# Flamingo block on Trainium2: the first layer's routing in two bursts, its scatters from iteration 18 on, the second routing and the weight fold moved to the attention's end and the first expert blocks

## The chip, the cores and the metric

The kernel runs on one core of a Trainium2 chip. The metric is the device time of one execution in microseconds (us); the times shown are medians of a few executions. Five engines work side by side and meet only at semaphores: TensorE (PE, matmuls), VectorE (DVE), ScalarE (ACT), GpSimd (POOL) and SyncE (SP), which issues most of the DMAs. Each engine runs its instructions in the order of its program, so a wait at the head holds up all that is queued behind it.

## The reference, cut to what matters

Two layers run on x of shape (128, 64, 128), 8192 tokens of 128 numbers, with a context of the same size. The change touches the first layer and the step from its attention to its experts:

```python
x = x + tanh(g_xattn[0]) * L0_xattn(layernorm(x), ctx)      # 16 heads of 8
# L0_ffn on layernorm(x): each token goes to its best 2 of 8 experts
logits = xt @ Wg + bg
scores = softmax(logits); topk_probs, topk_idx = top_k(scores, 2)
h = gelu(xt @ W1[e] + b1[e]); eo = h @ W2[e] + b2[e]
out = topk_probs[:, 0] * eo[topk_idx[:, 0]] + topk_probs[:, 1] * eo[topk_idx[:, 1]]
x = x + tanh(g_ffn[0]) * out
# layer 1: masked attention with one head, then experts that choose their 17 best tokens of each row of 64
```

All arithmetic shown is float32.

## The kernel before

**Tiles and parts.** The tokens are 64 tiles of 128. The first layer's expert stage treats them in three parts, tiles 0 to 23, 24 to 47 and 48 to 63. For each part the tokens are sorted by expert in DRAM: an indirect DMA per tile and per choice (`put`) writes the normalised rows to their places in `xg`, the expert blocks read `xg` in order, and indirect DMAs (`get`) fetch the results back. Part 0 has 17 blocks of 256 rows and 21 of 128.

**Attention of layer 0.** A loop over p = 0 to 34 treats two tiles in each iteration, as a pipeline of four stages. In iteration p PE does `scores(p)` and `attend(p-2)`, `spread_rden(p-3)`, `output(p-3)`; DVE does `largest(p)` (line 1173, the maximum over 128x2048), `normalise(p-3)` (1191), `shift(p)` (1179), `add_output(p-3)` (1197), `stats0` and `stats_router` (1164, 1169), `invert(p-2)` (1185). `scores(p+1)` needs the banks that `shift(p)` reads. ACT does the exponentials, copies the sums of stage p-2 (`copy_sums`, 1695), and at the end of iteration p normalises two tiles of group p//2+2 (`norm0`, 1709). SP moves the sums by DMA (`move_sums(p)`, 482 and 485), and behind them in iteration p it loads weights and writes two pieces of zeros (`fill`, 470) into `xg` and `odd`. There are 38 pieces, so the last two belong to p = 18. `move_sums(18)` waits for the sums that ACT copies in its iteration 20.

**POOL in that loop.** In an even p it spreads the keys of group p//2+1 (`keys`, 1973), which `scores(p+2)` reads; in every p it adds a bias to two tiles (`add_bias`, 1988); for p = 3, 7, 11, ... it computes mean and deviation (`moments_twice`, 1953 to 1963, and `moments`, 1928 to 1937); then come the puts (1999) of this p. `norm0(12)` in ACT's iteration 20 waits for the moments of POOL's iteration 19. Each `put` begins with

```python
                w.wait_ge(s_fill, 16 * fills)
                w.wait_ge(s_place, TOP * (h + 1))
```

**Routing.** `route0(h)` on DVE is a generator that the loop advances by hand: logits, softmax (its exponential on ACT), the two best experts, counts (`count0`, two matmuls on PE, copied by ACT), the block table, the place of each token, the expert of each block. Part 0 is routed in iterations 17 to 22 and its tiles are put in POOL's iterations 23 to 34; part 1 is routed in iterations 29 to 34 and put after the loop; part 2 is routed in the first expert blocks. The weights of layer 1 are folded on PE and DVE in iterations 33 and 34 (`output_bias`, `multiply_weights`, `fold_weights`).

**Expert blocks.** For each block PE turns the next unit's tokens (849), does `up0` (859) and, one block later, `down0` (869); DVE copies the turned tokens (1367), adds the bias (1386), in the small blocks copies weights (1377), and has steps of routing, of later rows (1158) and of combining between them.

Of the kernel before, what the change touches and what calls it, by code (L numbers as in the profile page):

```python
# [6 lines left out]

# [4 lines left out]
ALU = mybir.AluOpType  # L12
# [6 lines left out]
P = 128  # L19
# [60 lines left out]
UP_BANKS, DOWN_BANKS = (0, 1, 2, 5), (3, 6)  # L80
# [3 lines left out]
ROWS_FROM = 22  # L84
ROWS_BY = (3, 5, 6, 8, 9, 11, 12, 14, 15, 17, 20, PARTS[0][1])


def rows_by(p):

    return ROWS_BY[min(p - ROWS_FROM, len(ROWS_BY) - 1)] if p >= ROWS_FROM else 0  # L90
# [5 lines left out]
ROUTE1_FROM = 7  # L96

# [93 lines left out]
def build(nc, t_in, out):  # L191
    with ExitStack() as ctx:
# [106 lines left out]
        bias_rows = [ln1[:, 0, :], cut(9984, dict(d=D), "d")]  # L299
# [52 lines left out]
        def vec(name, n=1):  # L352
# [5 lines left out]
        BIAS_BANKS, ROUTER_BANKS = (0, 7), (1, 2, 3)  # L358
# [28 lines left out]
            "s_sm", "s_ex", "s_ch", "s_count", "s_counted", "s_place", "s_expert")]  # L387

# [41 lines left out]

        def routing_start(h):
            return 2 * (sum(PARTS[h]) // TG - 1) + 7
# [8 lines left out]
        def sync_program(e):  # L441
# [45 lines left out]

            filling = fill()
# [12 lines left out]
            def fetch_weights(b):  # L501
                _, h, j, _, _ = BLOCKS[b]
                w.wait_ge(s_expert, h + 1)
                number = e.value_load(expert[0:1, h, j:j + 1], min_val=0, max_val=NE - 1)
                w.wait_ge(ld["w1"], 16 * NE)
                w.wait_ge(s_hg, HC * (b - NW + 1))
                w.wait_ge(s_yb, b - NW + 1)
                e.dma_start(w1g(b), w1_sb[:, bass.ds(number, 1), :].rearrange("p a n -> p (a n)")
                            ).then_inc(s_w1g[b % NW], 16)
# [19 lines left out]
            w.wait_ge(s_sc, NP)  # L529
            w.wait_ge(s_kx, NG)  # L530
            for b in range(AHEAD):
                fetch_weights(b)
            for i in range(2):
                w.wait_ge(s_pt, 4 * (NP - 1 + i))
                half = slice(i * NE // 2, (i + 1) * NE // 2)
                load("w2", w2_sb[:, half], t_in["w2a"][:, half])
            w.wait_ge(s_bm, 2)
# [52 lines left out]
        def tensor_program(e):  # L590
# [8 lines left out]
            def output_bias(layer, weights):  # L599
                w.wait_ge(s_bv, layer + 1)  # L600
                wait_bank(BIAS_BANKS[layer])
                e.matmul(banks[BIAS_BANKS[layer]][:, 0:D], bias_rows[layer], weights, start=True, stop=True).then_inc(s_bm, 1)
                free[BIAS_BANKS[layer]] = s_bias_row, 2 * layer + 1
# [155 lines left out]
            def multiply_weights():  # L759
                w.wait_ge(s_wT, 1)  # L760
                w.wait_ge(ld["wo1"], 16)
                w.wait_ge(ld["vecs"], 32)
                wq, wk, wv = [ln_sb[:, ROUTER, n, :] for n in range(3)]
                e.matmul(banks[1][:, 0:D], wk, wq, start=True, stop=True)
                e.matmul(banks[1][:, D:2 * D], wv, wo1_sb[:], start=True, stop=True)
                e.matmul(banks[1][:, 2 * D:2 * D + 1], wk, vec("bq1"), start=True, stop=True)
                e.matmul(banks[1][:, 2 * D + 1:2 * D + 2], wq, vec("bk1"), start=True, stop=True).then_inc(s_fm, 1)

            def multiply_bias():
                w.wait_ge(s_fs, 1)  # L770
                e.matmul(banks[0][:, 0:1], cen[:], fold1[:, 2:3], start=True, stop=False)
                e.matmul(banks[0][:, 0:1], ln_sb[:, ROUTER, 3, :], vec("bk1"), start=False, stop=True).then_inc(s_fm, 1)
# [31 lines left out]
            for p in range(NP + 3):  # L804
# [3 lines left out]
                if 0 <= p - 2 < NP:  # L808
                    attend(p - 2)
                if p < NP:  # L810
                    values(p)
# [13 lines left out]
                for h in range(NPARTS - 1):  # L825
                    if p == routing_start(h) + 3:
                        count0(h)
# [8 lines left out]
                if p == NP:  # L836
                    turn_weights()
                if p == NP + 1:
                    output_bias(1, wo1_sb[:])
                    multiply_weights()  # L840
                if p == NP + 2:
                    multiply_bias()
# [19 lines left out]
            def down0(b, number):  # L862
# [3 lines left out]
                w.wait_ge(s_yb, b - 1)  # L866
                for n in range(cols // P):
# [8 lines left out]
            w.wait_ge(s_x1, NP)  # L876
            w.wait_ge(s_lg, NP)
            w.wait_ge(s_fs, 2)
            turn0(0)
            for b in range(NBL + 1):  # L880
# [9 lines left out]
                if b == 9:  # L890
# [54 lines left out]
            def route1(lo, turn_bank, bank):  # L945
# [28 lines left out]
                w.wait_ge(s_prob, NPARTS + k + 1)  # L974
# [104 lines left out]
        def vector_program(e):  # L1079
# [9 lines left out]
            def spread_bias(layer, bias):  # L1089
                w.wait_ge(ld["vecs"], 32)  # L1090
                w.wait_ge(s_ones, 1)
                if layer == 1:
                    w.wait_ge(s_kx, NG)
                e.tensor_scalar(bias_rows[layer], ones_row[:], bias, None, ALU.mult).then_inc(s_bv, 1)

            def output_bias(layer):
                w.wait_ge(ld["rows"], 16)
                w.wait_ge(s_bm, layer + 1)
                dst = (bias_sb, tbo_sb)[layer]
                e.tensor_tensor(dst[:], banks[BIAS_BANKS[layer]][:, 0:D], row_sb[:, layer, :], ALU.add).then_inc(s_bias_row, 1)  # L1100
# [30 lines left out]
            def fold_weights():  # L1131
                w.wait_ge(s_fm, 2)
                w.wait_ge(ld["vecs"], 32)
                step.then_inc(e.tensor_reduce(fold1[:, 0:1], banks[1][:, 0:D], AX_X, ALU.add))
                step.then_inc(e.tensor_copy(fold1[:, 2:3], banks[1][:, 2 * D + 1:2 * D + 2]))
                step.then_inc(e.tensor_scalar(ln_sb[:, ROUTER, 3, :], ones_row[:], vec("bq1"), 1.0 / D, ALU.mult, ALU.mult))
                step.done(e.tensor_scalar(w_sb[:, 6, :], banks[1][:, D:2 * D], TGX[1], None, ALU.mult))
                step.done(e.tensor_tensor(fold1[:, 1:2], banks[1][:, 2 * D:2 * D + 1], fold1[:, 0:1], ALU.subtract))
                step.done(e.tensor_scalar(fold1[:, 1:2], fold1[:, 1:2], 1.0 / D, None, ALU.mult))
                e.tensor_scalar(w_sb[:, 4, :], banks[1][:, 0:D], fold1[:, 1:2], None, ALU.add).then_inc(s_fs, 1)  # L1140

            def fold_bias():
                w.wait_ge(s_fm, 3)
                e.tensor_copy(fold1[:, 3:4], banks[0][:, 0:1]).then_inc(s_fs, 1)
# [56 lines left out]
            def softmax8(lo, n, call, dst=None):  # L1201
# [5 lines left out]
                w.wait_ge(s_ex, call + 1)  # L1207
                step.done(e.tensor_reduce(r, L, AX_X, ALU.add))
                step.done(e.reciprocal(r, r))
                e.tensor_tensor(L if dst is None else dst, L, bc, ALU.mult).then_inc(s_prob, 1)  # L1210
# [3 lines left out]
            def route0(h):  # L1214
                lo, n = PARTS[h]
                te = lambda buf: buf[:, 0:n * NE].rearrange("p (t e) -> p t e", e=NE)
                et = lambda buf: buf[:, 0:n * NE].rearrange("p (e t) -> p e t", t=n)
                r, tmp, left, total, upto = red[:, 0:n], te(tmp_sb), te(left_sb), et(total_sb), et(upto_sb)
                over = te(upto_sb)
                chosen = chosen_sb[:, 0:(TOP + 1) * n * NE].rearrange("p (k t e) -> p k t e", t=n, e=NE)  # L1220
                owner = owner_sb[:, 0:NBLK[h] * NE].rearrange("p (j e) -> p j e", e=NE)
                whole, whole_upto, end, first, large, small, small_upto, small_first, apart = [nb[:, k, :] for k in range(9)]
                by_tile = lambda v: v.unsqueeze(1).to_broadcast([P, n, NE])
                L = lg_sb[:, lo:lo + n, :]
                w.wait_ge(s_lg, (lo + n) // 2)
                w.wait_ge(s_lgx, (lo + n) // TS)
                w.wait_ge(ld["tables"], 96)
                w.wait_ge(s_momr, (lo + n) // TS)
                step.done(e.tensor_tensor(L, L, lgo_sb[:, lo:lo + n, :], ALU.add))
                step.done(e.tensor_tensor(L, L, rstd[:, lo:lo + n].unsqueeze(2).to_broadcast([P, n, NE]), ALU.mult))  # L1230
                step.done(e.tensor_tensor(L, L, small_sb[:, 0:1, :].to_broadcast([P, n, NE]), ALU.add))
                yield from softmax8(lo, n, h)
                bc = r.unsqueeze(2).to_broadcast([P, n, NE])
                order = small_sb[:, 1:2, :].to_broadcast([P, n, NE])
                for k in range(TOP):
                    src = L if k == 0 else left
                    step.done(e.tensor_reduce(r, src, AX_X, ALU.max))
                    step.done(e.tensor_scalar(gate0[:, k, lo:lo + n], r, TGF[0], None, ALU.mult))
                    step.done(e.tensor_tensor(tmp, src, bc, ALU.is_equal))
                    yield  # L1240
                    step.done(e.tensor_tensor(tmp, tmp, order, ALU.mult))
                    step.done(e.tensor_reduce(r, tmp, AX_X, ALU.max))
                    step.done(e.tensor_tensor(chosen[:, k, :, :], tmp, bc, ALU.is_equal))
                    if k == 0:
                        step.done(e.scalar_tensor_tensor(out=left, in0=chosen[:, 0, :, :], scalar=-2.0, in1=src,
# [934 lines left out]
```

## Time and profile before

| | us |
|---|---|
| median of 3 executions | 1024.92 |
| lowest and highest | 1023.31, 1031.78 |
| the profiled execution: its time | 1022.78 |
| the profiled execution: its span | 1021.0 |
| PE busy | 911.9 |
| POOL busy | 645.9 |
| DVE busy | 606.2 |
| ACT busy | 554.2 |

The span goes from the first instruction to the last; 1.8 us of the time lie outside. The attention of layer 0 fills the span up to about 300 us, the three parts of its experts 305 to 596, layer 1 the rest. Below, T with a number is the start of `largest` in that iteration: T17 is 143.33, T23 is 201.39, T31 is 262.30.

### The profile page before, as it was taken

The numbers are of one execution on the slowest core, as the hardware profiler recorded it, in microseconds if no ns is written. First come the engines' busy times: TensorE is split into PE (matmuls) and PEld (weight loads), VectorE is DVE, ScalarE is ACT, GpSimd is POOL, SyncE is SP. The second block draws the span as 40 slices with busy tenths as digits, with TensorE's granted clock in tenths as the row PEclk, the third lists the DMA queues.
The fourth block names the chain that finished last, engine by engine and source line by source line (L and its number), as shares of the span: only waits on it lengthen the run. The fifth ranks groups of instructions, "written<-read, shape, count | busy, mean of one in ns | idle before, by whom it ended". The sixth has DMA issues, their size and how long they took to land.

```text
span 1021.0 us, 24923 instructions
## 1 busy us (share of the span) xinstructions
PE 911.9 (89%) x8860; PEld 765.4 (75%) x8860; DVE 606.2 (59%) x1600; ACT 554.2 (54%) x1314; POOL 645.9 (63%) x804
## 2 busy tenths in 40 slices
PE   5999987798729999999999999978998999999991
PEld 3777775577519999899989988865776766878881
DVE  6887889999854554245625769984635324433320
ACT  2787876587405445444644766635555455444440
POOL 6353445378667777377427777721886758878885
PEclk9999999799859999999999999989999999999996
DMA  9364433022156656676566673141354635575453
GB/s 371 121 205 159 155 127 128 14 77 70 50 179 187 207 180 204 195 212 194 162 182 192 194 243 105 58 112 43 81 60 47 128 31 54 91 96 56 50 57 44
DMA packets 130154, 130.73 MB, mean 128 GB/s; under 512 B 32882, under 2 KB 102770, under 8 KB 129138
## 3 DMA queue, kind: packets, MB, share of 16 engines
q1 hardware_dynamic: 99810, 91.69, 28.5%
q0 software_dynamic: 28928, 29.91, 18.1%
q10 hardware_dynamic: 1296, 7.54, 1.8%
q8 instruction: 74, 1.21, 0.5%
q14 instruction: 46, 0.38, 0.1%
HBM read 53.88 MB, written 49.62 MB: 101 GB/s over the span
## 4 chain that ended last, share of the span: by engine, by line
PE 67%; DVE 13%; DMA 6%; issue 5%; ACT 4%; POOL 3%; SPq 1%; ACTq 0%; POOLq 0%; DVEq 0%
PE psum L859 12%; PE psum L869 12%; PE psum L1037 8%; PE psum L1027 8%; PE psum L665 4%; PE psum L652 3%; PE psum L682 2%; PE psum L991 2%; DMA odd<-ln_sb,dest 2%; DMA out_x<-ln_sb,dest 2%; PE psum L849 2%; DVE w_sb L1179 2%; DVE mx L1173 1%; PE psum L703 1%; POOL odd L2089 1%
## 5 line engine op out<-in xcount | busy, mean ns | idle before, releaser
L1793 ACT ACTIVATE hid_sb<-psum,work 128x128 f32<-128x128 f32 (+1 forms) x424 | 145.6, 412 | 144.7 <-PE psum L859 142.0
L2013 POOL DMA_INDIRECT work<-yg,place x128 | 122.9, 960 | 75.3 <-DMA yg<-yg_sb 36.3
L859 PE MATMUL psum<-work 128*128 128x128 f32 (+1 forms) x848 | 150.5, 321 | 2.3 <-issue 2.2
L869 PE MATMUL psum<-w_sb,hid_sb 128*128 x1192 | 150.2, 275 | 0.0
L869 PEld LDWEIGHTS psum<-w_sb,hid_sb 128*128 128x128 f32 x1192 | 144.8, 192 | 2.1
L1027 PE MATMUL psum<-work,w_sb 128*128 128x272 f32 (+2 forms) x512 | 130.6, 396 | 5.0 <-ACT ctx_sb L1895 3.1
L2089 POOL DMA_INDIRECT out_x<-ln_sb,dest x68 | 106.1, 1560 | 44.6 <-DVE ln_sb L1602 25.1
L859 PEld LDWEIGHTS psum<-work 128*128 128x128 f32 x848 | 124.5, 193 | 10.9 <-issue 3.8
L1895 ACT ACTIVATE ctx_sb<-psum,w_sb 128x272 f32<-128x272 f32 (+2 forms) x256 | 116.0, 488 | 25.6 <-PE psum L1027 21.9
L1037 PE MATMUL psum<-ctx_sb,w_sb 128*128 128x272 f32 (+2 forms) x512 | 128.1, 392 | 0.0
L1999 POOL DMA_INDIRECT xg<-work,place x104 | 100.8, 969 | 40.6 <-issue 24.9
L2089 POOL DMA_INDIRECT odd<-ln_sb,dest x68 | 105.7, 1555 | 32.2 <-issue 18.1
L1027 PEld LDWEIGHTS psum<-work,w_sb 128*128 128x128 f32 x512 | 92.1, 189 | 31.9 <-ACT ctx_sb L1895 8.5
L1386 DVE TENSOR_TENSOR yg_sb<-psum,work 128x128 f32<-128x128 f32 (+1 forms) x106 | 36.5, 345 | 120.5 <-PE psum L869 119.9
L1973 POOL TENSOR_SCALAR work<-work,vec_sb 128x512 f32<-128x512 f32 x64 | 43.6, 699 | 100.0 <-ACT work L1669 66.2
L1037 PEld LDWEIGHTS psum<-ctx_sb,w_sb 128*128 128x128 f32 x512 | 92.1, 190 | 15.5 <-issue 0.2
L1587 DVE TENSOR_SCALAR work<-psum,b2T_sb 128x272 f32<-128x272 f32 (+6 forms) x96 | 36.0, 403 | 93.0 <-PE psum L1037 93.0
L1863 ACT COPY work<-psum 128x272 f32<-128x272 f32 x64 | 24.8, 388 | 116.2 <-PE psum L991 115.8
L1688 ACT ACTIVATE work<-psum 128x512 f32<-128x512 f32 x128 | 70.2, 595 | 28.7 <-PE psum L665 28.5
L1173 DVE TENSOR_REDUCE mx<-psum 128x32 f32<-128x2048 f32 x32 | 73.3, 2290 | 19.8 <-PE psum L652 19.6
L1602 DVE TENSOR_TENSOR ln_sb<-psum,slot_sb 128x256 f32<-128x256 f32 (+1 forms) x64 | 28.2, 441 | 86.9 <-PE psum L1048 86.6
L1179 DVE TENSOR_TENSOR w_sb<-psum,mx 128x2048 f32<-128x2048 f32 x32 | 73.0, 2280 | 0.1
(254 smaller groups left out, 1631.6 us busy)
## 6 DMA issues: line engine op xcount, KB each, us to landing
work<-w_sb SPq DMA_DIRECT2D x76, 322.0 KB
work<-xg SPq DMA_DIRECT2D x73, 128.0 KB
yg<-yg_sb SPq DMA_DIRECT2D x73, 128.0 KB
xg<-yg_sb SPq DMA_DIRECT2D x24, 384.0 KB, 4.1
ctx_sb<-tok SPq DMA_DIRECT2D x8, 1088.0 KB, 6.7
ctxn<-sums_sb SPq DMA_DIRECT2D x64, 64.0 KB
out_x<-x_sb SPq DMA_DIRECT2D x16, 256.0 KB
odd<-yg_sb SPq DMA_DIRECT2D x10, 384.0 KB, 3.2
```

The costliest lines, as they stand in the source:

```text
L859: e.matmul(banks[UP_BANKS[c]][:, 0:cols], w1g(b)[:, c * P:c * P + P], xgT_sb[:, u % 2, at:at + cols], start=True, stop=True).then_inc(s_up, 1)
L869: ins = e.matmul(banks[DOWN_BANKS[b % 2]][:, n * D:n * D + D], hid0[:, b % 2, c, n * P:n * P + P], w2_sb[:, bass.ds(number, 1), c, :].rear ...
L1027: e.matmul(banks[b][:, 0:m * SLOTS], w1_sb[:, ex, c * P:c * P + P], xgT[sg % 2][:, ex, 0:m, :].rearrange("p t s -> p (t s)"), start=True, ...
L1037: ins = e.matmul(banks[3][:, 0:SIZES[sg] * SLOTS], w2_sb[:, ex, c, :], hid[:, ex % 2, c, 0:SIZES[sg], :].rearrange("p t s -> p (t s)"), st ...
L1173: e.tensor_reduce(mx[:, p % 2, :], four_banks, AX_X, ALU.max).then_inc(s_mx, 1)
L1179: e.tensor_tensor(pr[:, i, :, :, :, :].rearrange("p j u h k -> p (j u h) k"), four_banks, mx[:, i, :].unsqueeze(2).to_broadcast([P, 2 * HE ...
L1688: e.activation(dst, banks[B_T[half]], ACT.Exp, scale=SCALE0).then_inc(s_pT, 1)
L1793: e.activation(hid0[:, b % 2, c, 0:cols], banks[UP_BANKS[c]][:, 0:cols], ACT.Gelu, bias=w1g(b)[:, HID + c:HID + c + 1]).then_inc(s_hg, 1)
L1895: e.activation(hid[:, ex % 2, c, 0:m, :].rearrange("p t s -> p (t s)"), banks[(HC * ex + c) % 3][:, 0:m * SLOTS], ACT.Gelu, bias=w1_sb[:, ...
L1999: e.indirect_dma_start(xg_dram[h], at, src, None).then_inc(s_put[i], 16)
L2013: e.indirect_dma_start(dst[:, k, :], None, yg_dram[h], at).then_inc(s_get[i], 16)
L2089: e.indirect_dma_start(sum_rows[n % 2], at, yr[:, n % RESULTS, i, :], None, compute_op=ALU.add, bounds_check=NT * P - 1).then_inc(s_add1[n ...
```

## The change

- **Routing of part 0.** The top 2 are chosen on logits from which the maximum is subtracted; the softmax before the choice is gone. POOL adds up the logits of part 0 in iteration 15 (`add_logits`). DVE chooses in one burst at the end of iteration 16 (`choose0`, 12 instructions), counts and places in a second burst at the end of 17 (`runs0`, `places0`, 30 instructions), and finds the experts of the blocks at the end of 23 (`owners0`).
- **Puts.** The tiles of part 0 are put from POOL's iteration 18 on: tile 0 in 18, then 0, 2, 2, 1, 0, 2, 2, 1, 1, 2, 2, 2, 1, 3 and 2 tiles in 19 to 33.
- **Routing of part 1** starts in iteration 31 (1, 2, 1 and 1 steps in 31 to 34), is counted in 34, and ends in the expert blocks 0 to 4. Part 2 follows in blocks 5 to 8 and 12 to 17. The gates of all tiles are made together in block 18 (`gates0`), from one exponential in block 12.
- **Weight fold.** `turn_weights` and `multiply_weights` come earlier on PE, `fold_weights` on DVE in iteration 34; `multiply_bias` and the output bias come in expert block 1, in bank 3. The down banks of even and odd blocks are swapped.
- **SP.** Half of w2 (`load_down(0)`) and the first block's weights are fetched before `move_sums(30)`, the other half and two more blocks' weights after the last `move_sums`. The wait for `s_bm` before the first tokens is gone.

The diff, cut to its core:

```diff
+LOGITS_IN = 15
+COUNT_IN = LOGITS_IN + 2
+PUT_FROM = 18
+PUT_BY = (1, 1, 3, 5, 6, 6, 8, 10, 11, 12, 14, 16, 18, 19, 22, PARTS[0][1])
...
+    return min(PARTS[0][1], put_by(p + 1) + 1) if p + 1 >= PUT_FROM else 0
...
+ROUTE_IN = {NP - 1: 1, NP: 2, NP + 1: 1, NP + 2: 1}
+ROUTE_AT = {0: 1, 1: 1, 2: 1, 3: 1, 4: 1, 5: 1, 6: 1, 7: 1, 8: 1, 12: 1, 13: 1, 14: 1, 15: 1, 16: 1, 17: 1}
+COUNT_AT, SOFTMAX_AT, GATES_AT = 11, 12, 18
...
             for p in range(NP):
+                if p == NP - 2:
+                    load_down(0)
+                    w.wait_ge(s_sc, NP)
+                    w.wait_ge(s_kx, NG)
+                    fetch_weights(0)
                 move_sums(p)
...
+            load_down(1)
+            for b in range(1, AHEAD):
                 fetch_weights(b)
...
-            w.wait_ge(s_bm, 2)
...
+            def choose0(h):
...
+                if h == 0:
+                    w.wait_ge(s_logits, 1)
...
+                step.done(e.tensor_reduce(r, L, AX_X, ALU.max))
+                step.done(e.tensor_tensor(L, L, spread(r), ALU.subtract))
+                yield
+                step.done(e.scalar_tensor_tensor(out=tmp, in0=L, scalar=0.0, in1=order, op0=ALU.is_equal, op1=ALU.mult))
...
+                if p == LOGITS_IN + 1:
+                    for _ in choose0(0):
+                        pass
+                if p == COUNT_IN:
+                    for _ in chain(runs0(0), places0(0)):
+                        pass
+                if p == COUNT_IN + 6:
+                    for _ in owners0(0):
+                        pass
+                if p == NP + 2:
                     fold_weights()
+                for _ in range(ROUTE_IN.get(p, 0)):
+                    next(side)
                 for t in range(rows_by(p - 1), rows_by(p)):
                     put_rows(t)
...
             rows = later_rows(PARTS[1][0], NT)
+            copy_tokens(0)
+            w.wait_ge(s_put[0], 32 * (PARTS[0][1] // 4))
+            spread_bias(vec("bv_layer1"))
             for _ in range(TG):
                 next(rows)
-            copy_tokens(0)
...
+                if b == 1:
+                    fold_bias()
+                    output_bias(1)
...
                 if h == 0:
...
+                    for _ in range(ROUTE_AT.get(b, 0)):
+                        if next(side, True):
+                            side = route0(NPARTS - 1)
+                            next(side)
+                    if b == GATES_AT:
+                        gates0()
...
+                if p == LOGITS_IN:
+                    add_logits(*PARTS[0])
-                for t in range(rows_by(p - 2), rows_by(p - 1)):
+                for t in range(put_by(p - 1), put_by(p)):
                     put(t)
```

## Rows read from the trace of the kernel before

**Rows 1.** Windows by iteration: busy time of PE, PEld, DVE, ACT, POOL, then clock.

```profile
120.46:127.43 6.97, 6.79 (x153) 5.44 (x149) 6.25 (x10) 5.88 (x14) 2.23 (x4) 1.00 0.36 139
143.33:151.27 7.94, 7.53 (x207) 6.04 (x201) 7.80 (x14) 6.34 (x15) 1.94 (x3) 1.00 0.61 234
...
190.61:201.39 10.78, 8.61 (x69) 5.57 (x71) 9.84 (x20) 5.00 (x10) 5.29 (x12) 0.53 0.05 15
...
253.11:262.30 9.19, 7.63 (x138) 6.30 (x139) 8.98 (x15) 4.59 (x12) 7.76 (x11) 0.81 0.18 61
...
279.87:293.88 14.01, 3.84 (x18) 3.15 (x18) 10.45 (x39) 0.78 (x3) 6.65 (x7) 0.62 0.70 259
293.88:305.00 11.12, 1.93 (x9) 1.87 (x9) 3.80 (x13) 1.56 (x2) 8.83 (x15) 0.50 0.21 67
```

**Rows 2.** The chain that ended last, 293 to 307 us: start, us, what.

```profile
293.88 0.43 DVE ctxn L1191
...
300.44 2.24 DMA xg<-work,place
...
306.92 3.41 PE psum L859 x8
```

**Rows 3.** Timeline of DVE, part 0's routing: start, us, line, operation, tiles.

```profile
150.61 0.35 DVE L1204 TENSOR_REDUCE red<-lg_sb 128x24 f32<-128x192 f32 x1
151.00 0.36 DVE L1205 TENSOR_TENSOR lg_sb<-lg_sb,red 128x192 f32<-128x192 f32 x1
...
177.35 0.77 DVE L1252 COPY total_sb<-counts 128x192 f32<-128x192 f32 x1
...
182.79 2.28 DVE L1179 TENSOR_TENSOR w_sb<-psum,mx 128x2048 f32<-128x2048 f32 x1
...
194.58 0.18 DVE L1290 CAST place<-place_f 128x24 uint32<-128x24 f32 x1
```

**Rows 4.** Timeline of SP in iteration 18, and the landing of the zero fills.

```profile
170.62 1.35 SPq L482 DMA_DIRECT2D den_sb<-sums_sb  x2
...
174.32 0.91 SPq L470 DMA_DIRECT2D odd<-yg_sb  x2
...
DMA to landing us min/median/max: 2.1/3.8/8.0
```

**Rows 5.** Timeline of ACT in a plain iteration, T15 being 127.43.

```profile
127.16 0.90 ACT L1709 ACTIVATE ln_sb<-x_sb,nmr,rstd 128x128 f32<-128x128 f32 x2
128.42 0.59 ACT L1695 COPY sums_sb<-psum 128x512 f32<-128x512 f32 x1 [0.35 <-PE psum L682]
```

**Rows 6.** Timeline of POOL, single operations and the first and last puts.

```profile
159.53 0.25 POOL L1953 TENSOR_TENSOR work<-stats 128x16 f32<-128x16 f32 x1
...
164.96 0.49 POOL L1963 TENSOR_TENSOR nmr<-work,rstd 128x8 f32<-128x8 f32 x2
...
173.83 2.71 POOL L1973 TENSOR_SCALAR work<-work,vec_sb 128x512 f32<-128x512 f32 x4 [8.38 <-issue]
...
216.84 0.72 POOL L1988 TENSOR_TENSOR x_sb<-x_sb,bias_sb 128x256 f32<-128x256 f32 x1
...
261.73 0.34 POOL L1928 TENSOR_TENSOR work<-stats 128x8 f32<-128x8 f32 x1
265.79 0.30 POOL L1937 TENSOR_TENSOR nmr<-work,rstd 128x8 f32<-128x8 f32 x1
...
306.06 1.11 POOL L1999 DMA_INDIRECT xg<-work,place  x1 [0.58 <-POOL nmr L1937]
...
406.50 0.96 POOL L1999 DMA_INDIRECT xg<-work,place  x1 [0.30 <-issue]
```

**Rows 7.** DMA issues between 262 and 306 us: KB each, us to landing.

```profile
w_sb<-in_w2a SPq DMA_DIRECT2D x2, 1024.0 KB, 6.6
```

**Rows 8.** Expert blocks: window of the 17 large ones, the first get.

```profile
306.70:370.00 63.30, 62.66 (x415) 57.93 (x414) 33.56 (x115) 31.81 (x71) 48.07 (x51) 0.97 0.62 190
...
423.38 0.99 POOL L2013 DMA_INDIRECT work<-yg,place  x1 [15.92 <-DMA yg<-yg_sb]
```

More of the change, by code:

```diff
@@ L6 @@
 from contextlib import ExitStack
+from itertools import chain
 import numpy as np
@@ L1230, in route0 @@
[L1230 to L1245, printed above, removed]
-                                                         op0=ALU.mult, op1=ALU.add))
-                        yield
@@ L1249, in route0, with runs0 @@
                 yield
+            def runs0(h):
+                n = PARTS[h][1]
+                et = lambda buf: buf[:, 0:n * NE].rearrange("p (e t) -> p e t", t=n)
+                total, upto = et(total_sb), et(upto_sb)
+                whole, whole_upto, end, first, large, small, small_upto, small_first, apart = [nb[:, k, :] for k in range(9)]
                 w.wait_ge(s_counted, h + 1)
@@ L1285, in route0 @@
+                step.done(e.tensor_tensor(over, over, by_tile(APART), ALU.mult))
+                step.done(e.scalar_tensor_tensor(out=left, in0=by_tile(FIRST_ROW), scalar=float(LARGE), in1=left, op0=ALU.mult, op1=ALU.add))
                 step.done(e.tensor_tensor(left, left, over, ALU.add))
@@ L1292, in route0, with gates0 @@
                 yield
-                w.wait_ge(ld["tables"], 96)
-                for v, a, m in ((end, 0, NLARGE[h]), (small_upto, NLARGE[h], NSMALL[h])):
-                    step.done(e.tensor_tensor(owner[:, a:a + m, :], v[0:1, :].unsqueeze(1).to_broadcast([1, m, NE]),
-                                              block_sb[:, 0:m].unsqueeze(2).to_broadcast([1, m, NE]), ALU.is_le))
-                step.done(e.tensor_reduce(owner_sum[:, 0:NBLK[h]], owner, AX_X, ALU.add))
-                e.tensor_scalar(expert[:, h, 0:NBLK[h]], owner_sum[:, 0:NBLK[h]], float(NE - 1), None, ALU.min).then_inc(s_expert, 1)
-                w.wait_ge(s_expert, h + 1)
-                yield
+            def route0(h):
+                yield from choose0(h)
+                yield from runs0(h)
+                yield from places0(h)
+                yield from owners0(h)
+            def gates0():
+                first, second = gate0[:, 0, :], gate0[:, 1, :]
+                w.wait_ge(s_ex, 2)
+                step.done(e.tensor_reduce(first, lg_sb[:], AX_X, ALU.add))
+                step.done(e.reciprocal(first, first))
+                step.done(e.tensor_scalar(first, first, TGF[0], None, ALU.mult))
+                step.done(e.tensor_tensor(second, second, first, ALU.mult))
             step.done(e.memset(hid_sb[:], 0.0))
@@ L1338, in vector_program @@
                     add_output(p - 3)
-                for _ in range(steps[1]):
-                    next(side, None)
                 stats0(20 + 2 * p, 2)
@@ L1749, in scalar_program @@
                 g = p // 2 + 1
-                for h in range(NPARTS - 1):
-                    if p == routing_start(h) + 1:
-                        for _ in softmax8(*PARTS[h], h):
-                            pass
                 if 0 <= p - 2 < NP:
@@ L1855, in route1 @@
                     yield
[L1856 removed]
+                yield from softmax8(lo, NS, lo // NS)
             def copy_gathered(t, bank=4):
```

242 lines of the change are left out of this document (130 added, 112 removed).

## Prediction

> **What bounds the kernel now.** I read the page first: PE is busy 89% of the span, so what the change can win is time in which PE stands still. Then the windows, one for each iteration of the attention loop. A plain iteration takes 6.97 us, with PE busy 6.79 and DVE 6.25 [rows 1]: PE bounds it and DVE has about 0.7 us to spare. The iterations with routing go over to DVE: T17 to T23 take 58.1 us instead of 41.8, so part 0's routing costs 16.3 us; of part 1's the one shown takes 9.19, and the one ahead of it, from 243.5, 9.6: 4.8 us too much together. The last two windows take 25.1 us with PE busy 5.8 [rows 1]. The chain of waits says why [rows 2]: `normalise(31)` starts only at 293.88, since fold and placing are ahead of it on DVE; the last put lands at 302.7, the token fetch follows, and `up0(0)` starts at 306.92. From there PE is busy 62.66 of 63.3 us [rows 8]: a gain in the start of the blocks is a gain in the end, as the later stages follow each other with PE as the bound.
>
> **Routing of part 0, on DVE's path.** A burst at the end of an iteration delays `largest`. It is free for the 0.7 us of slack; the rest is paid.
> - `choose0` is 12 instructions. They take 0.39 us each from start to start (150.61 to 151.00) [rows 3], so 4.6 us; paid 3.8. T17 goes from 143.3 to 147.1. The three logit additions, which POOL takes over, are 1.1 us less on DVE.
> - `runs0` and `places0`: in the trace they stretch from 177.35 to 194.76, 17.4 us, among which lie two `largest`, one `shift` (2.2 to 2.3 each) and 1.7 of smaller work: 9.0 us are theirs [rows 3]. With two rows (0.5) and 6.3 of plain work T18 becomes 147.1 + 15.9 = 163.0, against 151.3.
> - In this burst PE has about 4 us of work and then stands some 8. In the window 190.6 to 201.4 the granted clock is 0.53 after such a wait, which is 1.2 GHz for most of it, and the next window is at 2.4 again; from `normalise` (ending 195.2) to the next `largest` (201.4) it took 6.2 us instead of 4.3. I charge 1.9 us once: T19 is 171.8, T20 178.7.
> - The sum so far: 199.7 against 201.4 at T23, as iterations 19 to 22 are plain. `owners0` in 23 costs 1.2. The two bursts alone are worth 0.5 to 1.5 us.
>
> **The early puts, and what is late in their place.** POOL reaches `put(0)` in its iteration 18 at about 170.6 (keys 2.7 and bias 0.7 behind the keys' arrival) [rows 6]. `put` waits for all zero fills, and the last two are issued by SP in iteration 18, behind `move_sums(18)`, which waits for ACT's iteration 20. The last one starts 4.2 us after SP's first DMA of that iteration (170.62 to 174.8, the second of the pair) [rows 4]. In a plain iteration the sums are copied by T+1.6 [rows 5]. So it starts at T20 + 5.8 = 184.5 and lands 3.8 later (median; 2.1 to 8.0): at 188.3. POOL stands 17.7 us. Before, it did not matter, as the first put came at 206.5.
>
> Queued behind that put are `add_bias(19)`, the moments of iteration 19, `keys(11)`. The moments take 5.9 us (159.53 to 165.4) [rows 6]. `norm0(12)` on ACT is due at T21 - 0.3 = 185.4 [rows 5], and it gets its moments at 188.3 + 2.5 (put) + 0.7 + 5.6 = 197.1. Behind it on ACT is `copy_sums(19)`, due at T21 + 1.0, on which `spread_rden`, `normalise` and `shift(21)` wait: 11 us of stall, 12.5 with a second stretch at 1.2 GHz. T31 becomes 255.3 + 7 + 7 = 269.3, where without this stall it would be 257 (before: 262.3).
>
> **POOL then sets the end of the puts.** From 188.3 it has 48 DMAs of 1.265 us (306.06 to 406.50 is 79 of them in 100.4 us; 60.7 us), five `keys` of 2.7, thirteen `add_bias` of 0.72, moments of 5.9 twice and 4.4 twice [rows 6]: 60.7 + 13.5 + 9.4 + 20.6 = 104.2 us, and 1 us of gaps. The last put is issued by 293.5 and lands 2.2 later [rows 2], at 295.7 instead of 302.7: 7.0 us earlier.
>
> **The tail, the other path.** With fold and places gone from iteration 33, DVE's own chain is: T31 + 9 end of 31; sums by DMA 3.6 us from issue, twice; `normalise(31)` at T31 + 20; fold (1.9) and one step (1.0); ready for `copy_tokens(0)` at T31 + 25.5 = 294.8. This is 2 us ahead of the tokens, so it hides. `up0(0)` is at 306.9 - 7.0 = 299.9. Unseen in the trace is a sums DMA behind 1.3 MB on SP's queue (`load_down(0)`, w1): between nothing and 6.6 us, the landing of such a load [rows 7]; it can be queued only behind what is left of it, and I take 1 us, covered by the 2 above.
>
> The Trainium skill (DMA: Bandwidth & Descriptors, Queues, rings and completion order) says that within a ring descriptors are consumed in the order of issue, which speaks against this move. By it the sums of stage 30 would wait for the whole of the load and the blocks would begin up to 5 us later than in my sum; no row of before has a large load ahead of the sums at the loop's end, so the trace neither confirms nor denies it.
>
> **Expert blocks.** Block 1 gets six small matmul passes of fold and bias; a pass of a whole `up0` block at the low clock is 3.41 / 8 = 0.43 us [rows 2], so they are 1.3 at most after the clock is up. DVE has 33.6 of 63.3 us busy [rows 8]; part 1's rest adds 9 us in blocks 0 to 4. A block lasts 3.73; a step of six 128x192 instructions (2.5), two copies (0.8) and two rows (0.6) is 3.9 to 4.0 and may hold PE by 0.3 in two blocks; `gates0` (about 1.5 in a block of 1.9) by up to 1. I charge 2.5 in all, between 1 and 6. The exponential with its table loads only changes its block. The puts of part 1 begin when places are written in block 3, about 318 instead of 306, and all end by 419 instead of 407.5; the gets begin at 423.4 now, on results that come 4 us earlier [rows 8], so this just hides.
>
> **Sum.** 7.0 - 2.5 = 4.5 us. On the profiled execution's 1022.8 that is 1018.3; the median of the three runs is 2.1 above that execution, and I set the forecast against it: 1020.4.
>
> **Rivals.**
> 1. **The fill is no obstacle**, or the stall behind it is shorter (fills land early, or ACT has slack). Then T31 is 257, POOL keeps up, the tail ends at T31 + 28 = 285.5, 21.4 us earlier, minus 2.5 to 4: 17 to 19 us, 1006 to 1008. For it: POOL has idle stretches in this loop, 8.4 us before a `keys` [rows 6]. Against it: the order on SP and the wait in `put` stand in the code, and iteration 20 comes after the place burst in either kernel.
> 2. **PE stays at 1.2 GHz** after the burst of 9 us and the stall. Place: iterations 18 to 24. Price: PE's 6.8 us become 13.6, so 6.6 us for each iteration that stays low. It decides from one such iteration on (the 1.8 us of cover and 4.5 of gain are gone); three give 1034. Against it: the window after 190.6 to 201.4 is back at 1.00 [rows 1]. The Trainium skill (TensorE: Matmul & The Clock Gate, Part 1) has the array return to full clock once it is busy again, by which this rival is not the likely one; the trace agrees, with 0.53 followed by 1.00.
> 3. **DVE bounds the first blocks**: each of the nine with a step held by 1 us or more instead of 0.3. Then 1026 to 1028, a little slower than before.
>
> **How the numbers follow.** The forecast, 1020.4 with its own range 1013 to 1027, has 0.60; rival 1 has 0.24; rival 2 0.08; rival 3 0.08. The range 1006 to 1028 leaves out rival 2 and the lower end of rival 1. Faster by over 1% (below 1014.7, about what measurement can tell) is rival 1 and the forecast's edge: 0.31. Slower by over 1% is rival 2: 0.07.
>
> **What would show it.** In the profile after: POOL idle for over 10 us before its first put, released by a DMA into `odd`, near 188; an ACT wait of about 10 us before line 1709's norm in iteration 20, by POOL's moments; one iteration of about 19 us; two stretches with a clock near 0.5; the last put of part 0 issued near 293 with POOL without idle before it; the first `up0` near 300. If there is no such wait, rival 1 holds. If the windows after 205 still show a clock near 0.5, rival 2. If PE idles between the large blocks, released by DVE's copies, rival 3.

## The result, and the profile after

The changed kernel takes 1028.31 us (median of 20 executions, 1026.27 to 1031.83) against 1024.82 for the kernel before (20 executions): a ratio of 1.0028, 95% interval 1.0014 to 1.0041. It is slower by 0.28%. The forecast was 1020.4, with a range of 1006 to 1028. The profiled execution of after is the slowest of its twenty (span 1030.0), so stages are compared here from points inside the span, above all from T15, the start of `largest` in iteration 15 (127.43 before, 128.12 after), and not from ends. The two profiled executions differ by 9.05 us, the medians by 3.5: the stages below add up to the first, and what is one execution's own can't be told from them.

In the kernel after, `largest` is line 1195, `shift` 1201, `normalise` 1213, the put 2065, the get 2079, the fill 483, `turn0`, `up0` and `down0` 865, 875 and 891.

Windows by iteration: T14 to T15 (plain), T16 to T17 (the choice in a burst), T17 to T18 (runs and places in a burst), T21 to T22, T22 to T23; columns as in [rows 1].

```profile
121.12:128.12 7.00, 6.82 (x153) 5.47 (x152) 6.26 (x9) 5.68 (x13) 2.22 (x4) 1.00 0.33 128
...
136.22:149.25 13.03, 10.76 (x233) 8.22 (x225) 11.38 (x22) 9.58 (x21) 5.70 (x9) 1.00 0.35 121
149.25:168.54 19.29, 11.49 (x142) 8.57 (x142) 16.02 (x43) 6.40 (x14) 3.48 (x5) 0.72 0.24 94
190.34:212.36 22.02, 8.06 (x150) 6.39 (x146) 6.70 (x10) 5.99 (x15) 14.92 (x23) 0.69 0.17 59
212.36:219.33 6.97, 6.79 (x153) 5.44 (x149) 6.06 (x7) 5.79 (x14) 5.82 (x7) 1.00 0.22 71
```

Three iterations are long, and the one from 190.34 stands out: 22.02 us in which PE is busy for 8.06, DVE for 6.70 and ACT for 5.99, so none of the three bounds it. The timelines of POOL, SP, ACT and PE around it, in this order, say what does:

```profile
167.81 0.72 POOL L2045 TENSOR_TENSOR x_sb<-x_sb,bias_sb 128x256 f32<-128x256 f32 x1
195.28 1.26 POOL L2065 DMA_INDIRECT xg<-ln,place  x1 [26.75 <-issue]
```

```profile
184.97 1.35 SPq L495 DMA_DIRECT2D den_sb<-sums_sb  x2
...
188.67 0.91 SPq L483 DMA_DIRECT2D odd<-yg_sb  x2
```

```profile
204.11 0.88 ACT L1765 ACTIVATE ln_sb<-x_sb,nmr,rstd 128x128 f32<-128x128 f32 x2 [13.91 <-POOL nmr L2020]
204.90 0.56 ACT L1751 COPY sums_sb<-psum 128x512 f32<-128x512 f32 x1
```

```profile
205.60 0.66 PE L712 MATMUL psum<-ident,rden_rows 128*128 128x128 f32 x2 [13.73 <-ACT sums_sb L1751]
206.06 1.91 PE L681 MATMUL psum<-ident,w_sb 128*128 128x128 f32 x8
```

POOL stands idle from 168.5 to 195.28, with the put at the head of its queue. The view calls the cause "issue", since the wait of a put is for several semaphores. What is late is the last zero fill, the second of the pair that SP issues from 188.67 on, behind the sums of stage 18 (184.97); the put is released some 6 us after it. A kernel of the experiments below (part 1 routed early), which is the same up to iteration 28, has the same wait, and there the view names the fill:

```profile
195.03 1.26 POOL L2065 DMA_INDIRECT xg<-ln,place  x1 [29.00 <-DMA odd<-yg_sb]
```

Behind the put, in POOL's order, are the moments; behind these on ACT are the norm and the sums of stage 19, and PE stands for 13.73 us. The second PE row is `turn_p` at 1.91 us for 8 matmuls, which take 1.04 where the granted clock is 1.00 (139.58 to 140.62): after this stand PE starts at 1.2 GHz.

From 195.28 to 304 POOL's longest pause is 0.52 us. The chain of waits from 270 us to the last put runs through POOL alone, puts above all and one set of moments, where before it ran through DVE [rows 2]:

```profile
299.54 2.24 DMA xg<-work,place
301.86 2.14 DMA work<-xg
...
306.16 3.41 PE psum L875 x8
```

The large blocks then fill [rows 8]'s window as follows, and below are the first put of part 1, the last put of all, and the first get.

```profile
305.95:370.00 64.05, 63.36 (x413) 57.95 (x413) 36.83 (x132) 31.19 (x69) 33.34 (x35) 0.96 0.56 170
```

```profile
326.30 1.11 POOL L2065 DMA_INDIRECT xg<-work,place  x1 [21.70 <-DVE work L1180]
...
427.17 0.96 POOL L2065 DMA_INDIRECT xg<-work,place  x1 [0.31 <-DMA xg<-work,place]
430.82 0.99 POOL L2079 DMA_INDIRECT work<-yg,place  x1 [2.69 <-DMA yg<-yg_sb]
```

The get used to come after 15.92 us of idle POOL, waiting for its data [rows 8]. Now it waits 2.69 and comes right behind the last put, 7.4 us later than before. The view names a `yg` DMA, but `get` waits for two things: the last results of part 0, which are the 28th write of `yg`, and every put. Before, that write was issued at 420.36 and the get followed 3.0 us later. In after it is issued here, 7.0 us ahead of the get and before the last put:

```profile
423.79 0.50 SPq L550 DMA_DIRECT2D yg<-yg_sb  x1
```

So what the first get waits for is the last put. In DVE's order, combining waits for the gets, and PE for DVE:

```profile
444.94 0.74 DVE L1441 SCALAR_TENSOR_TENSOR x_sb<-work,gate,x_sb 128x128 f32<-128x128 f32 x2 [2.50 <-DMA work<-yg,place]
```

```profile
446.28 0.41 PE L865 MATMUL psum<-ident,work 128*128 128x128 f32 x2 [1.26 <-DVE work L1414]
```

### The profile page after: what moved, and what is told of

It is laid out like the page before. It is cut to its first block, busy times and chain, and to the rows that moved or that the text cites. A ratio compares the mean times of both kernels' runs of the same rounds, so it can differ in the third digit from the quotient of the medians.

```text
span 1030.0 us, 24902 instructions
## 1 busy us (share of the span) xinstructions
PE 914.8 (89%) x8860; PEld 766.7 (74%) x8860; DVE 600.3 (58%) x1580; ACT 554.7 (54%) x1313; POOL 647.7 (63%) x807
## 4 chain that ended last, share of the span: by engine, by line
PE 64%; DVE 10%; DMA 7%; issue 7%; POOL 6%; ACT 4%; SPq 1%; ACTq 0%; POOLq 0%; DVEq 0%
PE psum L875 11%; PE psum L891 11%; PE psum L1060 8%; PE psum L1050 8%; PE psum L681 4%; PE psum L668 3%; PE psum L1014 2%; PE psum L698 2%; POOL xg L2065 2%; DMA odd<-ln_sb,dest 2%; PE psum L865 2%; POOL odd L2157 1%; ACT sums_sb L1751 1%; PE psum L719 1%; DMA x_sb<-in_x 1%
## 5 line engine op out<-in xcount | busy, mean ns | idle before, releaser
L875 PEld LDWEIGHTS psum<-work 128*128 128x128 f32 x848 | 125.0, 193 | 14.2 <-issue 6.8
```

The costliest lines, as they stand in the source:

```text
L875: e.matmul(banks[UP_BANKS[c]][:, 0:cols], w1g(b)[:, c * P:c * P + P], xgT_sb[:, u % 2, at:at + cols], start=True, stop=True).then_inc(s_up, 1)
```

## The experiments

Theory A: the wait at the first put is what turned the change from a gain into a loss. Theory B: the bursts cost more than their instructions. Theory C: the late puts and gets of part 1 and DVE's steps in the first blocks slow the expert stage. The table has all of them. "Loop" is T15 to T31, "first block" T15 to the first `up0` in PE's timeline, "experts" the first `up0` to the last `turn0`, each from one profiled execution; the last two columns are the median and the ratio to before, which ran beside each kernel (its medians lay between 1023.9 and 1025.4). How far one execution can be trusted, the table shows itself: the three spread kernels without a burst have the same program up to T31, and their loops are 125.0, 126.3 and 126.6. "Spread" means part 0's routing one step at a time, "tail filled" that steps of part 1 go where DVE is idle at the end of the loop.

| kernel | loop | first block | experts | us | ratio, 95% interval |
|---|---|---|---|---|---|
| before | 134.9 | 179.3 | 282.6 | 1024.8 | |
| after | 147.6 | 177.8 | 290.3 | 1028.3 | 1.0028 (1.0014 to 1.0041) |
| early fills | 131.7 | 162.0 | 286.1 | 1013.8 | 0.9883 (0.9847 to 0.9918) |
| first put in 21 | 132.0 | 165.3 | 288.5 | 1016.1 | 0.9910 (0.9876 to 0.9943) |
| spread | 125.0 | 164.9 | 287.1 | 1015.9 | 0.9902 (0.9866 to 0.9938) |
| spread, choice in a burst | 129.4 | 168.4 | 286.8 | 1020.8 | 0.9962 (0.9936 to 0.9989) |
| part 1 routed early | 151.5 | 183.1 | 285.5 | 1030.9 | 1.0057 (1.0034 to 1.0080) |
| the same, early fills | 135.2 | 165.7 | 284.2 | 1015.1 | 0.9904 (0.9875 to 0.9933) |
| spread, tail filled | 126.3 | 165.2 | 286.4 | 1013.8 | 0.9889 (0.9856 to 0.9923) |
| spread, tail filled, bias | 126.6 | 166.0 | 283.3 | 1013.6 | 0.9888 (0.9854 to 0.9922) |
| early fills, tail filled, bias | 132.0 | 162.5 | 283.8 | 1010.5 | 0.9855 (0.9820 to 0.9889) |

Some runs fell on chips where before itself took 1244 to 1248 us; the kernels were run again elsewhere, except the control, and what those chips showed stands in the last section.

**Early fills.** Both kernels got this edit:

```diff
-                for _ in range(2):
+                for _ in range(2 if p < NE else 4):
                     next(filling, None)
```

> After, with the zero fills issued earlier: SP issues two pieces per iteration up to p = 7 and four from p = 8, so all 38 are out by p = 13. Theory A (POOL's wait for the last zero fill at put(0) is what costs the time: it holds the moments, ACT's norm and sums, PE): POOL no longer waits 26.75 us, T21 to T22 falls from 22.0 to about 7, T31 from 275.7 to about 261, the first up0 from 306.2 to 288 to 292, and the time is 12 to 18 us under after: 1010 to 1016. Rival B (the stall is only the cover of another bound: the bursts on DVE and the 60 us of puts on POOL need that time anyway): T31 falls, but the first up0 stays within 3 us of 306 and the time is 1025 to 1028. Rival C (the late gets of part 1 set the end): the first block moves, but the end of the experts moves by 5 us or less.

Measured where before takes 1023.9: 1013.76. POOL's first put now waits for a row that DVE normalises, 1.75 us:

```profile
165.53 1.26 POOL L2065 DMA_INDIRECT xg<-ln,place  x1 [1.75 <-DVE ln L1180]
```

```profile
187.32:194.23 6.91, 6.50 (x150) 5.11 (x146) 6.55 (x10) 5.77 (x14) 5.80 (x7) 1.00 0.21 69
```

T21 to T22 is a plain iteration of 6.91 us instead of 22.02, the loop 15.9 us shorter, the first block 15.8 and the time 14.6. Theory A holds, B and C as rivals to it fall. (The experts are 4.2 us shorter as well in these two executions.) The control:

> Before with the early zero fills, the control, again on a chip where before takes about 1025. Theory A (only the wait at the first put of after is at stake; before's first put comes long after the last fill has landed): within 1 us of before, 1023.5 to 1025.5. Rival (fills beside the sums and puts cost time by themselves): 3 us or more faster.

It ran twice, both times on a chip of that kind: 0.9995 (0.9959 to 1.0031) and 1.0011 (0.9978 to 1.0044) against before. There, moving the fills is worth nothing by itself, within 0.4%. On a chip where before takes 1025, where the 14.6 us were gained, the control was not measured; the next kernel takes their place.

**First put in iteration 21**, fills and bursts untouched, the other way to remove the wait:

```diff
-PUT_BY = (1, 1, 3, 5, 6, 6, 8, 10, ...
+PUT_BY = (0, 0, 0, 3, 5, 6, 8, 10, ...
```

> The same kernel as after_put21 (after, first put in POOL's iteration 21, bursts and late fills kept), again on such a chip. Theory A: the wait is 3 us or less and hides, T21 to T22 is under 9 us instead of 22.0, T31 is 130 to 135 us behind T15 instead of 147.6; POOL has some 92 us of work from 193 on, so the first up0 is 163 to 168 us behind T15 (after: 177.8): 1015 to 1019. Rival B (POOL's amount of puts is the bound, wherever they start): the first up0 is within 3 us of after's and the time above 1025.

Measured 1016.11, with a wait of 2.81 us at the first put, T21 to T22 6.57 us and the first block at 165.3. As theory A has it, by a second way that leaves the fills where they are; and the three tiles that early fills let POOL put in iterations 18 to 20 are worth only 3.3 us in the first block.

**The bursts undone.** Part 0's routing one step at a time, puts from 23; all else as in after, late fills too.

```diff
-COUNT_IN = LOGITS_IN + 2
+COUNT_IN = 20
+ROUTE0_IN = {16: 1, 17: 1, 18: 1, 19: 1, 20: 1, 21: 2, 22: 2}
-PUT_FROM = 18
+PUT_FROM = 23
```

> After, with both bursts undone: part 0's choice, runs and places one step each in iterations 16 to 20 and two in 21 and 22, counts in 20, owners in 23, puts from iteration 23 in before's numbers; the fills are late as in after, and everything else of the change stays. Theory A: no put waits for a fill (they are out by about 190, the first put comes at about 200), so T21 to T22 is under 11. Theory B (the two bursts cost 5 us more than their instructions, through PE at the low clock behind them): T23 is 198 to 200 against 219.3 in after and 201.45 with early fills and bursts, so that the bursts are worth 1 us against or nothing; T31 is 258 to 260, puts end at 293 to 297 by POOL's own work, the first up0 is 298 to 302 and the time 1020 to 1025. Rival E (bursts are better than steps by more than 2 us): T23 is 204 or more.

Measured 1015.94. T23 is 68.5 us behind T15 (in absolute terms 197.13), against 75.4 with early fills and bursts and 74.0 before. No put waits for a fill (0.73 us at the first one, for moments), as theory A has it. Theory B was still too mild, and its 1020 to 1025 missed: by T23 steps are 7 us cheaper than bursts, and rival E is reversed. The first block comes 2.8 us later than with bursts and early fills, since POOL gets its puts later, and DVE stands 13.19 us before the first tokens:

```profile
292.50 0.42 DVE L1412 COPY work<-psum 128x256 f32<-128x256 f32 x1 [13.19 <-PE psum L866]
```

Then the choice alone as a burst:

```diff
-COUNT_IN = 20
-ROUTE0_IN = {16: 1, 17: 1, 18: 1, 19: 1, 20: 1, 21: 2, 22: 2}
+COUNT_IN = 17
+ROUTE0_IN = {16: 4, 18: 1, 19: 1, 20: 1, 21: 1, 22: 1}
```

> The spread kernel with the choice (12 instructions) as a burst at the end of iteration 16 again, counts in 17, and the five steps of runs and places one each in iterations 18 to 22. Between T15 and T31 the spread kernel takes 125.0 us, that with both bursts (and early fills) 131.7. Theory B1 (the burst of runs and places, 9.4 us in which PE runs dry and starts at the low clock again, is what costs): T16 to T17 is 13, but T31 is 125 to 128 behind T15 and the time within 2 us of 1015.9. Theory B2 (the burst of the choice costs as much of itself): T31 is 129 or more behind T15, the time 1018 or more.

Measured 1020.82, the loop 129.4: theory B2. I had taken the second, longer burst for the dear one. The first costs 4.4 us of the 6.7 between spread and both bursts, or 2.8 to 3.1 if the other two kernels with the spread loop are taken; at T23, where the three spread kernels agree within 0.6, it is 71.5 us behind T15 against 68.2 to 68.7. Its rows in this kernel, of DVE and then of PE:

```profile
146.24 0.73 DVE L1258 SCALAR_TENSOR_TENSOR tmp_sb<-lg_sb,small_sb 128x192 f32<-128x192 f32 x1
...
147.82 0.77 DVE L1261 SCALAR_TENSOR_TENSOR left_sb<-chosen_sb,lg_sb 128x192 f32<-128x192 f32 x1
...
149.39 0.36 DVE L1265 TENSOR_TENSOR tmp_sb<-tmp_sb,small_sb 128x192 f32<-128x192 f32 x1
```

```profile
153.51 1.00 PE L720 MATMUL psum<-wo_sb,ctxn 128*128 128x136 f32 x4 [3.45 <-DVE ctxn L1214]
154.30 1.92 PE L682 MATMUL psum<-ident,w_sb 128*128 128x128 f32 x8
156.01 1.43 PE L808 MATMUL psum<-chosen_sb,before_sb 128*128 128x192 f32 x4
```

PE runs dry for 3.45 us, comes back at 1.2 GHz, `turn_den` is late, behind the counts (line 808) as well, and DVE waits 1.73 us for it in the next iteration. T16 to T18 takes 21.6 us, 7.6 more than two plain iterations, for 5.5 us of DVE work. The four iterations 16 to 19 of the spread kernel hold the same four steps of DVE and take 31.2, 3.3 more than plain; but the counts, which PE makes in 17 here, come there in 20, so not all of the difference is the burst's.

**Part 1 routed earlier**, in iterations 29 to 34, so that its puts can follow part 0's:

```diff
-ROUTE_IN = {NP - 1: 1, NP: 2, NP + 1: 1, NP + 2: 1}
-ROUTE_AT = {0: 1, ..., 8: 1, 12: 1, ..., 17: 1}
+ROUTE_IN = {NP - 3: 1, NP - 2: 1, NP - 1: 2, NP: 1, NP + 1: 2, NP + 2: 2}
+ROUTE_AT = {0: 1, ..., 4: 1, 12: 1, ..., 17: 1}
```

> The same kernel as route1 (after, with part 1 routed in iterations 29 to 34 and counted in 32), again on a chip where before takes about 1025. Its loop is still held by POOL's wait at the first put, and DVE's extra steps hide behind the puts. Theory C: part 1's puts follow part 0's without a gap from about 301, the first get is 114 to 119 us behind the first up0 instead of 124.9, part 1's blocks lose their 3.2 us of delay, and the time is 3 to 6 us under after: 1022 to 1025. Rival (the delay comes from the matmuls of fold and bias and from gates0): within 1.5 us of after, 1027 to 1030.

Measured 1030.91. The experts take 285.5 us instead of 290.3, 4.8 less: theory C is right on what the late puts and the steps cost. But the loop grew by 3.9 (3.6 of it between T29 and T31) and the first block by 5.2, as these iterations are bound by DVE and not by POOL; that the steps hide was wrong, and so were the 1022 to 1025. With early fills:

> After with the early zero fills, and part 1 routed in iterations 29 to 34 (steps 1, 1, 2, 1, 2, 2) with its counts in iteration 32, instead of 31 to 34 and blocks 0 to 4. Theory C (the late puts and gets of part 1 and DVE's steps in the first blocks cost some 7 us between the first block and the end of the experts): part 1's puts start at 290 to 295 instead of 307.6, the first get at 396 to 402, blocks 1 to 8 lose their holds, and the time is 3 to 6 us under that of the early fills alone, which was 1013.8: 1008 to 1011. Rival D (the steps are only moved: iterations 29 to 31 are bounded by DVE and give back in the loop what the blocks gain): the first up0 is 4 to 6 us later than 288.05 and the time is within 2 us of 1013.8.

Measured 1015.10: experts 1.9 us shorter, first block 3.6 later (T15 itself is 2.6 later in this execution), rival D. Theory C's first get at 396 to 402 was far off: it came at 413.16, 8.77 us of idle POOL behind the last put, when part 0's results were there.

**The idle end of the loop filled.** In the spread kernel four steps of part 1 go where DVE stood 13.19 us, and then also the bias work of block 1 (DVE's part of the edit; PE's matmuls move ahead of the first `turn0` with it, and blocks 0 to 3 lose their steps):

```diff
             rows = later_rows(PARTS[1][0], NT)
+            w.wait_ge(s_bm, 2)
+            fold_bias()
+            output_bias(1)
+            w.wait_ge(s_bias_row, 3)
+            step.done(e.tensor_scalar(tbo_sb[:], tbo_sb[:], TGX[1], None, ALU.mult))
+            for _ in range(4):
+                next(side)
             copy_tokens(0)
```

> The spread kernel (bursts undone, puts from 23) with four more steps of part 1's routing (rest of runs, places) put in DVE's stream before it copies the first block's tokens, where DVE stood idle 13.19 us; they are taken out of blocks 0 to 3, and part 2's steps come four blocks earlier. Theory C (late puts of part 1 and the steps in the first blocks): the first up0 stays at 293 to 294, the first put of part 1 comes at 294 to 296 instead of 313.7, the first get is 116 to 119 us behind the first up0 instead of 124.3, and of the 4.5 us that the experts take longer than in before 2.5 to 3.5 go: 1012 to 1014. Rival (the steps are no burden where they are): within 1 us of 1015.9.

> The kernel before this one in the list, and also the fold's bias and layer 1's output bias made before the first block (DVE and PE stand idle there) instead of in block 1, with a row of their own as in before. Theory: block 1's extra matmuls and DVE's extra copies behind them hold the second and third block by 1.4 to 1.7 us; without them the step from the first to the second large block is as in before, 3.9 us, and the time 1 to 2 us less: 1011 to 1013. Rival: the slip in block 1 comes from DVE's other work (rows of part 1), and nothing changes.

Measured 1013.84 and 1013.58. The steps hide: the first block stays at 165.2. They gain 0.7 us in the experts where 2.5 to 3.5 were expected (2.6 at the end of part 1, of which 1.9 is lost again at part 2's start; I did not find out why). The table has 3.1 us in the experts for the bias work, but only 1.2 of them are there until the end of part 1: the fourth `turn0` comes 7.1 us behind the first `up0` instead of 8.3. The other 1.9 are just what the kernel without it had lost at part 2's start, where PE waits 0.62 us for tokens here and 1.33 there. The kernels differ at that place by up to 3 us, also where no edit touches it, so they are not shown to be the bias work's. In the time it is 0.3 us: T15 is 1.1 later in this execution, the first block 0.9 later behind it, and the end of the experts has another bound by then. PE's timeline there, this kernel and then the one without:

```profile
585.09 0.63 PE L629 MATMUL psum<-ident,ln_sb 128*128 128x128 f32 x4 [1.73 <-DVE yg_sb L1432]
```

```profile
585.11 0.63 PE L628 MATMUL psum<-ident,ln_sb 128*128 128x128 f32 x4 [0.54 <-DVE yg_sb L1431]
```

1.2 of the 3.1 us go into the longer wait. DVE's last combining waits for gets, which POOL issues every 1.25 us without a pause from 562.09 to 581.37:

```profile
583.88 0.74 DVE L1440 SCALAR_TENSOR_TENSOR x_sb<-work,gate,x_sb 128x128 f32<-128x128 f32 x2 [1.08 <-DMA work<-yg,place]
```

**The same on the early fills**, with two steps, as DVE had only 5.09 us there:

> The same kernel as fill_tail_bias, again on a chip where before takes about 1025. Theory C: the first up0 stays 162 to 163 us behind T15, from the first up0 to the last turn of the experts 283.5 to 285 us instead of 286.1: 1010 to 1012.5. Rival F (POOL's gets are the bound at the end of the experts): PE waits 1.5 us or more for DVE's last results ahead of layer 1, and the time is within 1 us of 1013.8.

Measured 1010.46, ratio 0.9855: the best of all, 1.45% under before and by the two ratios 1.7% under after. The first block is at 162.5 and the experts take 283.8, both as theory C has it. Rival F has its wait, 1.84 us ahead of layer 1, but not its time; the early fills alone wait 1.69 there, so this edit added next to nothing to it.

## Why the prediction was wrong, by its own steps

The forecast was a gain of 4.5 us: 7.0 at the first block, less 2.5 in the blocks. The mechanism of the largest loss, the late fill, was named with its place and came. Two steps failed. POOL's first put came 7.0 us later than in the sum, so that the first block gained 0.8 us and not 7.0; and the blocks lost 7.7 us and not 2.5, mostly because the late puts, which were to "just hide", did not. Together that turns the gain into a loss.

- **"`choose0` … 4.6 us; paid 3.8" and "T19 is 171.8".** T15 to T19 should take 44.4 us and took 48.1. The choice took 5.5 us (143.75 to 149.25), above all because two of its operations took 0.73 and 0.77 us; and PE's return at 1.2 GHz, charged once, came behind each burst. The slow ones lie beside POOL's `keys` and `add_bias` (142.37 to 146.77). The spread kernel has the same two operations while POOL is idle (147.1 to 156.78), and a third one, which took 0.36 in after with POOL idle, beside `add_bias`:

```profile
151.36 0.29 DVE L1258 SCALAR_TENSOR_TENSOR tmp_sb<-lg_sb,small_sb 128x192 f32<-128x192 f32 x1
...
152.47 0.36 DVE L1261 SCALAR_TENSOR_TENSOR left_sb<-chosen_sb,lg_sb 128x192 f32<-128x192 f32 x1
...
159.75 0.77 DVE L1265 TENSOR_TENSOR tmp_sb<-tmp_sb,small_sb 128x192 f32<-128x192 f32 x1
```

```profile
159.44 1.66 POOL L2043 TENSOR_TENSOR x_sb<-x_sb,bias_sb 128x256 f32<-128x256 f32 x2
```

  The Trainium skill (SBUF — State Buffer, SBUF: two separate sides) has DVE operations with two inputs in SBUF and GpSimd's operations take one pair of ports in turn; the trace agrees, with 0.29 and 0.36 us for the first two once POOL is idle. The 0.39 us of the sum came from a stretch in which POOL was idle.
- **"It starts at T20 + 5.8 … and lands 3.8 later".** The start was right: the second of the pair starts at T20 + 5.8, 0.5 behind the row at 188.67. The put was released about 6 us later, inside the 2.1 to 8.0 of [rows 4]; for the last of a row of transfers, for which everything waits, the median was too small. T21 to T22 became 22.0 instead of 19.5. The first put came at 195.28 instead of 188.3: 0.7 us at T15 already, 4.0 from T15 to T20, 2.3 by the landing.
- **"POOL then sets the end of the puts".** Right, and its 104 us as well (195.28 to 300.5, 105.2). What was late ahead of it went into its end: the last put was issued at 299.54 instead of 293.5. The first `up0` is 0.8 us earlier in the chain (306.92 to 306.16) instead of 7.0.
- **"I charge 2.5 in all" for the blocks.** The experts took 7.7 us more. Where, the writes of `yg` tell: behind the first `up0`, the 21st (part 0) comes 3.8 us later than in before, the 51st (part 1) 7.1, the 66th (part 2) 7.7. The 51st in before, in after, and with part 1 routed early:

```profile
504.75 0.59 SPq L527 DMA_DIRECT2D yg<-yg_sb  x1
```

```profile
511.09 0.59 SPq L550 DMA_DIRECT2D yg<-yg_sb  x1
```

```profile
511.76 0.59 SPq L550 DMA_DIRECT2D yg<-yg_sb  x1
```

  With part 1 routed early, where the first `up0` is at 311.21, the three are 2.5, 2.5 and 2.9. So 4.8 of the 7.7 are DVE's steps in the first blocks (1.3) and the late puts and gets of part 1 (3.5). The bias work is 1.6 in part 0 and 1.2 in part 1 (the two kernels with the tail filled), near the 1.3 charged for it. The remaining 1 to 2 us have no experiment.
- **"so this just hides"** failed in kind and not only in size. The puts of part 1 begin at 326.30 and not at about 318, 6 of these 8 us by the late first block; the puts end 20.7 us later than before, not 11.5, and the first get waits for them and not for its data. Part 1's blocks lost 3.3 us. What a late get costs is not settled: with early fills it comes 123.4 us behind the first block and the loss is 0.5; in the spread kernel with the choice in a burst it comes at 124.9, as in after, and the loss is 1.4.
- **The tail.** `normalise(31)` started at T31 + 18.8 and DVE stood 5.32 us for the tokens: it hides, as forecast. Of the sums behind the load, PE waited 0.74 us for stage 30's, issued from 283.16 and used at 287.44 (4.3 us; stage 31's 2.8), so the delay was about 1.5 us, near my 1 us:

```profile
287.44 0.24 PE L706 MATMUL psum<-ident,den_sb 32*128 32x32 f32 x1 [0.74 <-DMA den_sb<-sums_sb]
```

  By the rule that I weighed there (the Trainium skill, DMA: Bandwidth & Descriptors, Queues, rings and completion order) it could have been 5; a wait of this kind is there in the trace, but small.
- **Rivals.** Rival 1 (T31 at 257) is what the kernel with early fills does: 257.70. It gives 1013.8 and not 1006 to 1008: POOL still ends the loop and the first block is at 288.05 instead of 285.5, and the blocks cost 3.5; the rest lies behind the last `turn0`, where its execution takes 4.8 us more than before's, 1.2 of it in the wait ahead of layer 1 (1.69 against 0.53) and 3.6 not explained. Rival 2 did not occur: three stretches have a low clock (0.72, 0.60 and 0.69 from T17, T18 and T21), and the window behind the last one shows 1.00. The Trainium skill (TensorE: Matmul & The Clock Gate, Part 1) had it so, and the trace agrees. Rival 3 had the right engine, DVE in the first blocks, for a part of the loss.

## What to carry to other kernels

Before an operation is moved earlier, list everything that its waits name, not only the one that the change serves: what was long done at the old place (here a zero fill that nobody waited for) may be the last to arrive at the new one, and an in-order queue hands the wait on to engines that have nothing to do with it. Work on an engine with 0.7 us of slack in each iteration was cheaper in pieces than in a burst, since the burst let PE run dry and come back slow. And once a stage gets shorter, look for the queue that was hidden behind it: POOL's puts and gets, at 1.25 us each, ended the loop, held the first get, and held DVE's last combining. Last, a gain read as the difference of two profiled executions can hold something else: of the bias work's 3.1 us 1.9 lay at a place where the kernels differ by as much without it.

## What the runs showed of the hardware

Three of the chips ran before in 1244 to 1248 us instead of 1025, with the same program. Up to the first put the one looked at is hardly slower: the kernel before with early fills reaches it at 208.76 us, before on the other kind of chip at 206.53. Nearly all of the 220 us come behind it. While POOL issues its puts (208.76 to 216.34), PE's timeline there shows groups of about five matmuls with pauses for which nothing in the profile is responsible; the same 64 matmuls take 1.10 us as one group beside the puts on the other kind of chip (208.32 in before). The rows are PE's and then POOL's:

```profile
210.92 0.32 PE L682 MATMUL psum<-work,hid_sb 128*32 128x64 f32 x5 [0.38 <-issue]
211.66 0.32 PE L682 MATMUL psum<-work,hid_sb 128*32 128x64 f32 x5 [0.42 <-issue]
212.40 0.32 PE L682 MATMUL psum<-work,hid_sb 128*32 128x64 f32 x5 [0.42 <-issue]
```

```profile
212.85 0.96 POOL L1999 DMA_INDIRECT xg<-ln,place  x1 [0.31 <-issue]
214.12 0.96 POOL L1999 DMA_INDIRECT xg<-ln,place  x1 [0.30 <-issue]
```

On such a chip the order of the kernels turns: early fills 1.0155 of before (1.0114 to 1.0196), first put in 21 1.0208 (1.0154 to 1.0261), part 1 early 1.0131 (1.0079 to 1.0183), and even the best kernel 1.0080 (1.0048 to 1.0111). After itself did not run there. What is slow there was not looked into, so the gains above hold for the other kind of chip alone.
